# Four graph layers on one core: every third block of the first layer's sums taken from gathered rows instead of weight tables

## The reference, cut to what matters

```python
h = jnp.maximum(_layernorm(x, axis=-1), 0.0)
msg = edge_val[:, None] * x[edge_src]          # x is h here, edge_val the edge weight
neighbor = jax.ops.segment_sum(msg, edge_dst, num_segments=N_NODES)
out = neighbor @ W1.T + b1 + (x * neighbor) @ W2.T + b2
```

## Time and profile before

| | us |
|---|---|
| median of 3 runs (lowest, highest) | 2557.92 (2553.99, 2568.24) |
| the profiled execution's own time | 2558.8 |
| its span in the trace | 2556.4 |
| TensorE busy | 2265.3 (89%) |
| VectorE busy | 1554.3 (61%) |
| ScalarE busy | 1235.4 (48%) |
| GpSimd busy | 133.9 (5%) |

### The profile page before, as it was taken

How to read it: one execution, slowest core, us unless ns; L and a number is a source line. 1 busy time by engine, 2 the same in 40 slices (tenths; PEclk the granted TensorE clock), 3 DMA queues, 4 the chain that set the end, 5 groups by cost and what they waited for, 6 DMA issues and landing times.

```text
span 2556.4 us, 58105 instructions
## 1 busy us (share of the span) xinstructions
PE 2265.3 (89%) x20263; PEld 2023.6 (79%) x20263; DVE 1554.3 (61%) x2760; ACT 1235.4 (48%) x3085; POOL 133.9 (5%) x114
## 2 busy tenths in 40 slices
PE   1599999999999999999987799999998426999897
PEld 1399999999999999999965566676787415888644
DVE  7677777777777777777745455555774582000133
ACT  4555555555555555555411577766886410000142
POOL 5300000000000000000000000000000340000000
PEclk7699999999999999999955899999999757999999
DMA  8222122112212212211233533233583147888221
GB/s 249 58 77 75 50 75 75 63 63 75 75 50 75 75 50 75 75 57 69 76 100 87 179 110 109 109 109 110 211 314 127 58 115 292 301 300 301 90 67 55
DMA packets 178788, 299.34 MB, mean 117 GB/s; under 512 B 13064, under 2 KB 130059, under 8 KB 178627
## 3 DMA queue, kind: packets, MB, share of 16 engines
q1 hardware_dynamic: 174592, 284.33, 32.2%
q0 software_dynamic: 4144, 14.34, 2.0%
HBM read 198.15 MB, written 100.49 MB: 117 GB/s over the span
## 4 chain that ended last, share of the span: by engine, by line
PE 82%; DVE 8%; DVEq 3%; issue 2%; ACT 2%; DMA 2%; ACTq 0%; POOLq 0%; POOL 0%; SPq 0%; PEldq 0%
PE ps L730 21%; PE ps L790 20%; PE ps L719 16%; PE ps L713 8%; PE ps L774 5%; PE ps L829 4%; PE ps L760 3%; PE ps L923 2%; DVE hT_s L1358 1%; DMA hs<-node_rows 1%; PE ps L820 1%; DVE carry L1554 1%; PE ps L837 1%; PE ps L960 0%; ACT edge_area L1010 0%
## 5 line engine op out<-in xcount | busy, mean ns | idle before, releaser
L1057 ACT CAST edge_area<-ps 128x392 f16<-128x392 f32 x784 | 385.5, 492 | 490.0 <-PE ps L713 490.0
L790 PE MATMUL ps<-big,rows_area 128*128 128x256 f16 (+1 forms) x4900 | 553.1, 274 | 24.8 <-DMA big<-edge_counts 24.8
L730 PE MATMUL ps<-big,rows_area 128*128 128x128 f32 x4802 | 571.3, 276 | 0.0
L730 PEld LDWEIGHTS ps<-big,rows_area 128*128 128x128 f32 x4802 | 550.9, 192 | 0.0
L719 PE MATMUL ps<-edge_area 128*128 128x196 f16 x4704 | 541.7, 250 | 0.0
L790 PEld LDWEIGHTS ps<-big,rows_area 128*128 128x128 f16 x4900 | 474.9, 99 | 82.8 <-DMA big<-edge_counts 25.1
L719 PEld LDWEIGHTS ps<-edge_area 128*128 128x128 f16 x4704 | 422.1, 97 | 0.3
L1063 ACT COPY big<-ps 128x392 f32<-128x392 f32 x784 | 384.5, 490 | 9.8 <-PE ps L719 1.4
L713 PE MATMUL ps<-edge_area 128*128 128x196 f16 x2352 | 334.4, 250 | 13.7 <-DVEq L1500 13.7
L1495 DVE TENSOR_TENSOR edge_area<-lo_pair,carry 128x768 f16<-128x768 f16 x392 | 218.7, 558 | 202.5 <-PE ps L719 124.1
L1496 DVE TENSOR_TENSOR edge_area<-cell_pair,carry 128x1176 f16<-128x1176 f16 x392 | 299.3, 764 | 0.0
(11 more groups left out here) (221 smaller groups left out, 1607.4 us busy)
## 6 DMA issues: line engine op xcount, KB each, us to landing
big<-edge_counts SPq DMA_DIRECT2D x336, 448.0 KB, 4.9
edge_counts<-edge_area SPq DMA_DIRECT2D x49, 1568.0 KB, 5.7
hs<-node_rows POOLq DMA_DIRECT2D x21, 448.0 KB, 4.5
x_stream<-edge_area SPq DMA_DIRECT2D x14, 448.0 KB, 3.9
node_rows<-edge_area SPq DMA_DIRECT2D x14, 448.0 KB, 3.0
edge_area<-x_stream SPq DMA_DIRECT2D x14, 448.0 KB, 3.9
node_rows<-rows_area SPq DMA_DIRECT2D x1, 3136.0 KB, 12.5
edge_area<-in_x SPq DMA_DIRECT2D x7, 448.0 KB, 4.7
```

Of the source, the lines that this page charges most:

```text
L730: last = mm(p_sum[par], h0[:, n, :], w32[:, par, n, :], start=(n == 0), stop=(n == NB - 1))
L790: last = mm(p_block[par][:, 0:width, :], planes[:, p, sh, :], piece[:, par, k, 0:width, j, :], start=(sh == 0 and p == 0), stop=(sh == NB ...
L1057: nc.scalar.copy(store_slot[:, par, :, cols], p_count[s % 2]).then_inc(sem("count_taken"), 1)
```

## The change

After half 0, the loops go in **sets** of three halves, 16 of them: 3t+1, 3t+2 and 3t+3. Halves 3t+1 and 3t+3 are done as before. In half 3t+2 only the counts are made. Its sum is taken from rows: the half has at most 4608 = 36 x 128 edges, in the edge list one behind the other; `load_set` on GpSimd fetches their records, 36 to a partition (an indirect DMA); `split_set` on VectorE takes source, destination and weight apart; `gather_set` fetches the source rows of `h`, 128 rows of 512 bytes with each of 36 indirect DMAs, in 12 bursts of 3, at most 4 bursts ahead of TensorE; VectorE makes for each burst a 128 x 3 x 128 one-hot of the destination in 32 bits (L1626) and multiplies it by the weight in place (L1635); TensorE multiplies the three tiles of rows by it (`add_edges`, L809), into a PSUM bank of its own. The two remaining `weigh`s of a set are cut in 12 pieces over the three halves. The `drain` behind a duo's last one-hot is gone; the semaphore rises with the instruction itself. Stores wait for the one before them. In the opening GpSimd makes a selection matrix, TensorE 4 more small matmuls, and VectorE 15 more small operations to find where each set begins. A flag that a half has more than 4608 edges joins those that choose the general path. Other edits only rename semaphores and move small tiles (`gain`, `last_clique`, and the gather's row buffers, which lie in `agg_s` and `hT_s`).

Cut to its core, eight columns of indent taken off:

```diff
+SETS = NHALF // 3
+SPAN = 36
+BURST = 3
+BURSTS = SPAN // BURST
+AHEAD = 4
+MADE = 2
...
     def store_half(h, b, par):
 
+        sp.wait_ge(sem("half_saved"), h * 16 + 32)
+        sp.sem_inc(sem("passed"), 1)
         sp.wait_ge(sem("count_taken"), h * SGS + SGS + 2)
         sp.dma_start(cells_dram[bass.ds(b, 1), :, :, par * PART:(par + 1) * PART].rearrange("o k p n -> p (o k) n"),
                      store_slot[:, par, :, :].rearrange("p (k n) d -> p k (n d)", k=SUBS)).then_inc(
-            sem(f"half_saved{par}"), 16)
+            sem("half_saved"), 16)
...
                             pattern=[[-1, P]], channel_multiplier=1).then_inc(sem("made"), 1)
+    pool.drain()
+    for j in range(4):
+        last = nc.gpsimd.tensor_copy(picker[:, j, :], ident[:, 32 * j:32 * j + 1].to_broadcast([P, P]))
+    last.then_inc(sem("made"), 1)
     for n, (first, last) in enumerate(TILES):
...
+    def load_set(t):
+
+        nc.gpsimd.tensor_copy(chunk_slot[:, 0:1], set_start[:, bass.ds(t, 1)])
+        pool.drain()
+        pool.indirect_dma_start(
+            out=set_rec[:].rearrange("p c r -> p (c r)"), out_offset=None, in_=rec_dram,
+            in_offset=bass.IndirectOffsetOnAxis(ap=chunk_slot[:, 0:1], axis=1),
+        ).then_inc(sem("set_in"), 16)
+
+    def gather_set(t):
+        pool.wait_ge(sem("set_split"), t + 1)
+        for burst in range(BURSTS):
+
+            pool.sem_inc(sem("passed"), 1)
+            pool.wait_ge(sem("edges_summed"), t * BURSTS + burst + 1)
+            pool.sem_inc(sem("passed"), 1)
+            for n in range(BURST):
+                c = burst * BURST + n
+                pool.indirect_dma_start(
+                    out=edge_row[c % (AHEAD * BURST)], out_offset=None, in_=rows_dram,
+                    in_offset=bass.IndirectOffsetOnAxis(ap=set_idx[:, c:c + 1], axis=0),
+                ).then_inc(sem(f"rows_in{burst % AHEAD}"), 16)
+            if burst == AHEAD + 1:
+
+                load_set(t + 1)
+
+    def gather_sorted():
+        load_set(0)
+        pool.wait_ge(sem("rows_written0"), 16)
+        with pool.Fori(0, SETS) as t:
+            gather_set(t)
+        pool.wait_ge(sem("set_in"), 16 * (SETS + 1))
...
-    def supergroup(h, s):
+    def supergroup(h, s, k=None):
...
+        if k is None:
+            return
+        pe.wait_ge(sem("weight_taken"), k * SGS + s + 1)
         for c in range(3):
             for oh in (oh_whi, oh_wlo):
                 last = mm(group_of(p_weight[s % 4], c), weights_of(oh, slot, r, c), cells_of(slot, r, c),
...
+    def add_edges(t, burst):
+        pe.wait_ge(sem(f"rows_in{burst % AHEAD}"), (t * (BURSTS // AHEAD) + burst // AHEAD + 1) * (16 * BURST))
+        pe.sem_inc(sem("passed"), 1)
+        pe.wait_ge(sem("edge_onehots"), t * BURSTS + burst + 1)
+        for n in range(BURST):
+            c = burst * BURST + n
+            last = mm(p_edges, edge_row[c % (AHEAD * BURST)], edge_oh[burst % MADE][:, n, :],
+                      start=(c == 0), stop=(c == SPAN - 1))
+        last.then_inc(sem("edges_summed"), 1)
+
+    def window(t):
+
         for s in range(SGS):
-            supergroup(h, s)
-            if weighed and s % 4 == 3:
-                hi = lo + (12 if s < SGS - 1 else 13)
-                weigh(h - 1, 1 - par, lo, hi)
-                lo = hi
+            supergroup(t * 3 + 1, s, t * 2 + 1)
+            if s % 4 == 3:
+                weigh(t * 2, 0, s // 4 * 8, s // 4 * 8 + 8, t * 3)
+                add_edges(t, s // 4)
+        for s in range(SGS):
+            supergroup(t * 3 + 2, s)
+            if s % 4 == 3:
+                if s < SGS // 2:
+                    weigh(t * 2, 0, *((32, 40), (40, NB))[s // 4], t * 3)
+                else:
+                    weigh(t * 2 + 1, 1, *((0, 8), (8, 17))[s // 4 - 2], t * 3 + 1)
+                add_edges(t, 4 + s // 4)
+        for s in range(SGS):
+            supergroup(t * 3 + 3, s, t * 2 + 2)
+            if s % 4 == 3:
+                weigh(t * 2 + 1, 1, 17 + s // 4 * 8, 25 + s // 4 * 8, t * 3 + 1)
+                add_edges(t, 8 + s // 4)
 
     def count_sorted():
         pe.sem_inc(sem("weight_ready"), 2 * RING)
         pe.sem_inc(sem("weighed"), 2)
-        half(0, 0, False)
+        pe.sem_inc(sem("edges_summed"), AHEAD)
+        for s in range(SGS):
+            supergroup(0, s, 0)
         pe.wait_ge(sem("h0_ready"), 2)
-        with pe.Fori(0, NHALF // 2) as i:
-            half(i * 2 + 1, 1)
-            half(i * 2 + 2, 0)
-        weigh(NHALF - 1, 0, 0, NB)
+        with pe.Fori(0, SETS) as t:
+            window(t)
+        weigh(2 * SETS, 0, 0, NB, 3 * SETS)
...
+    def take_edges(t):
+
+        act.wait_ge(sem("edges_summed"), t * BURSTS + BURSTS + AHEAD)
+        return nc.scalar.activation(agg[:, bass.ds((t * 3 + 2) * P, P)], p_edges, ACT.Copy)
+
+    def take_window(t):
         for s in range(SGS):
-            take_supergroup(h, par, i, s)
-            if s == 1 and summed:
-                take_sum(h - 2, par).then_inc(sem("sum_taken"), 1)
+            take_supergroup(t * 3 + 1, (t + 1) % 2, s, t * 2 + 1, 1)
+        for s in range(SGS):
+            take_supergroup(t * 3 + 2, t % 2, s)
+            if s == SGS // 2:
+                take_weighed(t * 3, t * 2).then_inc(sem("sum_taken"), 1)
+        for s in range(SGS):
+            take_supergroup(t * 3 + 3, (t + 1) % 2, s, t * 2 + 2, 0)
+        take_weighed(t * 3 + 1, t * 2 + 1).then_inc(sem("sum_taken"), 1)
+        take_edges(t).then_inc(sem("sum_taken"), 1)
...
+    V.tensor_copy(half_start, p_start)
+    V.tensor_scalar(lane_off, gbase[:, 0:1], float(SPAN * REC) / G, None, ALU.mult)
+    V.tensor_scalar(set_base, iota16[:, 0:SETS + 1], 3.0 * P, 2.0 * P, ALU.mult, ALU.add)
+    dve.drain()
+    for n in range(4):
+
+        j, g = (3 * n + 2) % 4, (3 * n + 2) // 4
+        begin = half_start[:, j, g:g + 10:3]
+        after = half_start[:, (j + 1) % 4, g + (j + 1) // 4:g + (j + 1) // 4 + 10:3]
+        V.tensor_scalar(set_start[:, n:SETS:4], begin, lane_off, float(NE * REC - SPAN * REC), ALU.add, ALU.min)
+        V.tensor_tensor(set_over[:, n:SETS:4], after, begin, ALU.subtract)
+    dve.drain()
+    V.tensor_copy(set_start[:, SETS:SETS + 1], set_start[:, 0:1])
+    V.tensor_scalar(set_over, set_over, float(SPAN * P * REC), None, ALU.is_gt)
...
-    def duo_onehots(duo, slot):
-
-        dve.wait_ge(sem("weight_ready"), duo * 2 + 2)
+    def duo_onehots(duo, slot, weighted=True, edges=None):
         key, lo, whi, wlo = (t[:, bass.ds(duo * 3, 3), :, :] for t in by_duo)
         V.tensor_tensor(oh_src[:, slot], paired(lo_pair, P), lo.to_broadcast([P, 3, P, 2]), ALU.is_equal)
-        V.tensor_tensor(oh_cell[:, slot], paired(cell_pair, CELLS), key.to_broadcast([P, 3, CELLS, 2]), ALU.is_equal)
-        dve.drain()
-        V.tensor_tensor(oh_whi[:, slot], oh_src[:, slot], whi.to_broadcast([P, 3, P, 2]), ALU.mult)
-        V.tensor_tensor(oh_wlo[:, slot], oh_src[:, slot], wlo.to_broadcast([P, 3, P, 2]), ALU.mult)
-        dve.drain()
-        dve.sem_inc(sem("onehots"), 1)
+        last = V.tensor_tensor(oh_cell[:, slot], paired(cell_pair, CELLS), key.to_broadcast([P, 3, CELLS, 2]),
+                               ALU.is_equal)
+        if not weighted:
+            last.then_inc(sem("onehots"), 1)
+        if edges:
+            t, burst = edges
+            of = [v[:, burst * BURST:(burst + 1) * BURST].rearrange("p (c o) -> p c o", o=1).to_broadcast(
+                [P, BURST, P]) for v in (set_dst, set_w)]
+            dve.wait_ge(sem("edges_summed"), t * BURSTS + burst + 1 + AHEAD - MADE)
+            V.tensor_tensor(edge_oh[burst % MADE], iota16[:, 0:P].rearrange("p (o d) -> p o d", o=1).to_broadcast(
+                [P, BURST, P]), of[0], ALU.is_equal)
+        if weighted or edges:
+            dve.drain()
+        if weighted:
+            V.tensor_tensor(oh_whi[:, slot], oh_src[:, slot], whi.to_broadcast([P, 3, P, 2]), ALU.mult)
+            V.tensor_tensor(oh_wlo[:, slot], oh_src[:, slot], wlo.to_broadcast([P, 3, P, 2]), ALU.mult).then_inc(
+                sem("onehots"), 1)
+        if edges:
+            V.tensor_tensor(edge_oh[burst % MADE], edge_oh[burst % MADE], of[1], ALU.mult).then_inc(
+                sem("edge_onehots"), 1)
...
+    def split_set(t):
+        dve.wait_ge(sem("set_in"), t * 16 + 16)
+        V.tensor_copy(set_idx, set_rec[:, :, 0])
+        V.tensor_copy(set_w, set_rec[:, :, 2])
+        dve.drain()
+        V.tensor_scalar(set_dst_i, set_idx, 6, None, ALU.arith_shift_right)
+        dve.drain()
+        V.tensor_scalar(set_idx, set_idx, 63, None, ALU.bitwise_and)
+        V.tensor_scalar(set_dst, set_dst_i, set_base[:, bass.ds(t, 1)], None, ALU.subtract)
+        dve.drain()
+        V.scalar_tensor_tensor(out=set_idx, in0=set_idx, scalar=float(P), in1=set_rec[:, :, 1], op0=ALU.mult,
+                               op1=ALU.add)
+        dve.drain()
+        dve.sem_inc(sem("set_split"), 1)
+
+    def onehot_window(t):
+        for j in range(DUOS):
```

(30 more changed lines are left out.)

190 lines of the change are left out of this document (107 added, 83 removed).

## The result

The changed kernel took **2663.16 us** (median of 4 runs, 2649.17 to 2667.2), the kernel before beside it 2559.09: a ratio of 1.0393, 95% interval 1.0344 to 1.0441. It is slower, outside my range and on the other side. Later the same kernel, unedited, was measured twice more, each time with the kernel before beside it: 2663.47 us (ratio 1.0407, 1.0381 to 1.0434) and **2431.8 us** (0.9507, 0.9478 to 0.9536). So there are two answers, and most of what follows is about what tells them apart.

What follows compares the result with a forecast made beforehand. TensorE was taken to bound the old kernel at 71.12 us a set; three engines near 62 us plus 1.9 and 1.2 gave 65. Sixteen sets gain 97.9 us, other terms leave -93.7: 2464 us, range 2412 to 2640.

Steps and rivals of the forecast that it cites:

- Together: Per set: three engines at about 62 us, plus 1.9 for VectorE held and 1.2 for a loop stall, 65 us.
- 59.7 to 61.7: TensorE's time per set in us: 59.7 of matmuls, up to 61.7 with waits for ScalarE's copies in the middle half.
- p: GpSimd's time per gather or record DMA, put at 1.5 us; a set takes 37 p + 6.9, 62.4 us.
- Rival (a): GpSimd becomes the bound: each DMA waits twice, p = 1.87, a set takes 76.1 us, 2642 us; chance 0.17.
- steps of 2.35 us: VectorE's time for a duo of one-hots without the second drain, 2.35 us against 2.78 before.
- +1.9: Per set, VectorE held when GpSimd reads: 0.05 us for each of 37 DMAs, 1.9 us.
- rival (c): A VectorE one-hot waits for a whole gather, 35 us a set: a set of 96 us, 2968 us; chance 0.08.
- The stall at the loop's branch: VectorE's longer loop may fetch instructions again once a round: one stall a set, 1.2 us.
- End: After the sets, VectorE's degree count no longer hidden by TensorE's last weigh: +3.5 us.
- Opening and half 0: 15 small VectorE operations in the opening, about +2.5 us; half 0, bound by VectorE, -1.8 us.
- my signs of being wrong: GpSimd's share passing that of the other two engines, or VectorE's steps keeping the old 0.35 us.

Runs made afterwards that it cites:

- late execution: Changed kernel, unedited, profiled in the result's series, where TensorE's signals reached other engines late: 2663.16 us, ratio 1.0393 to the kernel before.
- Regimes: Changed kernel with four sets each as changed, at most 6 gathers queued, plain transfers instead of indexed gathers, and two bursts ahead: 2605.41 us.
- quiet execution: Changed kernel, unedited, in a later series without late signals: 2431.8 us, ratio 0.9507 to the kernel before.
- vector_slot: Changed kernel with at most 6 gathers queued and VectorE, not GpSimd, copying the next record address: 2430.76 us, then 2428.51, and 2640.1 in a late-signal series.

## Why the prediction was wrong

- **What failed** is the step "Together": "Three engines at about 62 us. Two things add to it." The sum of engine times was taken as the time of a set, with a gain for every engine that stayed under it. Where the signals are late, none of the three sets the pace: a set took 78.5 us, not 65. Of the 15 above the quiet 63.3, some 5 are longer matmuls (TensorE busy 65.7 of 78.5 us by the two windows of the late execution, against 61.07) and some 10 are waits. Regimes shows, with its plain sets beside the others in one execution, that the indexed gathers make them. No rival of mine had a cost that is on no engine, so the range ended at the price of a slow GpSimd.
- **Where they are not late, the sum of the set held within 2 us**: 63.3 against 65. 16 x (71.12 - 63.3) = 125 us; measured 2557.82 - 2431.8 = 126. Forecast were 97.9 and 2464, range 2412 to 2640. That 125 and 126 agree so well is partly luck: against the one trace of the kernel before, the quiet one has its first `weigh` 7.6 us earlier and needs 7.2 us more behind the last, a stretch that takes 1276 to 1289 us in the traces without extra stores.
- **TensorE**, 59.7 to 61.7: busy 61.07 of 63.30 us. The middle half waits for ScalarE as estimated (2 us a set): in the waits view of the quiet execution, 35.0 us in 15 sets, 2.3 each.

```profile
PE ps L780 <- ACT edge_area L1150: 35.0, 79, 0.6
POOL set_rec L613 <- issue: 57.3, 15, 3.8
DVE edge_area L1616 <- issue: 12.7, 15, 0.9
```

- **GpSimd**: p = 1.43, not 1.5, and its own copy and drain cost 3.8 us a set instead of 0.5 (second line). Rival (a) is out; with four bursts of lead neither reached TensorE. vector_slot, which takes the second away and has the limit of six, is level with the change (2428.51 and 2431.8).
- **VectorE**: steps of 2.35 us and edge operations of 0.56 as forecast. The "+1.9" for holds by GpSimd didn't come: its one-hots are 0.55 and 0.76 long beside gathers too, so rival (c) is out. The stall at the loop's branch was forecast at 1.2 and is 0.85 (third line), but no instruction was fetched between 178 and 1140 us of that execution, so it is not a refetch. The 1.2 had been read from the earlier trace rows, and that was misread: stalls there belong to the late series, and the quiet ones have none. VectorE didn't set the end, so neither term counted: 63.3, not 65. The prediction also misapplied the page that it cites: by the Trainium skill ("Runtime: NRT & Kernel Launch", Instruction fetch mechanics) the refetch is for a target outside the current two pages, 512 instructions on most engines. The trace has 260 VectorE instructions in a round, and no fetch.
- **End**: I put +3.5. VectorE's degree count ended at 1146.4 in the quiet execution and TensorE's last `weigh` at 1147.8, so it stayed hidden: 0. **Opening and half 0**, compared within the kind of series of the kernel before's trace: the first one-hot comes at 106.3 us instead of 104.8, +1.5 where I put +2.5, and half 0 lasts 19.6 instead of 22.9, -3.4 where I put -1.8.
- None of my signs of being wrong came: GpSimd's share did not pass the others, the steps of VectorE lost the old 0.35, and TensorE did not wait at L809 for rows, the sign of (a). It waited at L780 for ScalarE, which waited for TensorE's own signal.

**What stays open**: why a series has late signals or not (four of nine measured did, counting that of the result), and by what way indexed gathers in a row delay TensorE's signals, and VectorE's instructions in the opening, but not the signals of ScalarE or VectorE. The trace of the late execution also lacks most records of the gathers' landings: it has 3134 of 9216, where the quiet one has 8970. So the writing of the trace's own records may take part. All runs here were profiled, and whether an unprofiled run has late signals was not tried. No version was found that beats the kernel before in both kinds of series: that one takes 2557 to 2562 us in all of them.

## What to carry to other kernels

Two engines that hand each other small buffers, two banks deep, live from signals of 0.04 us; price what new traffic could do to the signal, not only to the engines. A stall with no releaser in the trace of the kernel before, beside the kind of traffic that a change multiplies, is to be explained before it is priced. Before explaining an effect by its cures, run the unedited kernel again beside them: here every edit "cured" it. Where an effect comes and goes with the series, put the variants and their control in one program, in successive rounds of its loop.
